# Rounding the second layer's context and weights inside the first layer's loop

## The reference, cut to what matters

```python
def bitnet_linear(x, W, b):
    w_scale = jnp.maximum(jnp.mean(jnp.abs(W)), 1e-05)
    qW = jnp.sign(W) * (jnp.abs(W) > 0.5 * w_scale).astype(W.dtype)
    i_scale = jnp.maximum(jnp.max(jnp.abs(x)), 1e-08) / 127.0
    qx = jnp.clip(jnp.round(x / i_scale), -128.0, 127.0)
    out = jnp.einsum('...i,oi->...o', qx, qW) * (w_scale * i_scale)
    return out + b
...
vis = bitnet_linear(dinov2_features, W_d2v, b_d2v)
image_embeds = bitnet_linear(vis, W_img, b_img)
fused = bitnet_linear(text_embeddings, W_txt, b_txt)
for Wa, ba in ((W_att0, b_att0), (W_att1, b_att1)):
    kv = bitnet_linear(image_embeds, Wa, ba)
...
x = _layernorm(x + _L0_attn_ref(x, ...), axis=-1)
x = _layernorm(x + _L0_xattn_ref(x, ctx_768, ...), axis=-1)
```

## Time and profile before

| What | us |
|---|---|
| median of 3 runs | 2812.44 (2810.92 to 2817.76) |
| profiled execution, its own time | 2813.72 |
| its span in the profile | 2812.4 |
| stage one, start to last copy | 0 to 242 |
| inputs of stage two, to the first copy of the values | 242 to 365 |

### The profile page before, as it was taken

How to read it: one execution, slowest core, us unless ns; L and a number is a source line. 1 busy time by engine, 2 the same in 40 slices (tenths; PEclk the granted TensorE clock), 3 DMA queues, 4 the chain that set the end, 5 groups by cost and what they waited for, 6 DMA issues and landing times. The chain is left out here.

```text
span 2812.4 us, 41641 instructions
## 1 busy us (share of the span) xinstructions
PE 2188.7 (78%) x15624; PEld 1422.1 (51%) x15694; DVE 1672.9 (59%) x3413; ACT 1179.7 (42%) x2185; POOL 567.4 (20%) x489
## 2 busy tenths in 40 slices
PE   6993689896408999277779999995887696788677
PEld 3552157673406888234435555653555443455544
DVE  4666965468763333456666666643777642777663
ACT  2222844335232333032225555563666443566443
POOL 2110000001273455401220000001322131322052
PEclk9996689998657999578889999996998898899999
DMA  3005000100260111233321011102000001000000
GB/s 111 1 1 156 15 1 1 46 1 1 76 230 28 46 46 42 68 88 85 93 77 36 25 36 25 25 13 90 1 1 1 11 1 60 1 1 1 37 12 23
DMA packets 75074, 113.30 MB, mean 40 GB/s; under 512 B 22916, under 2 KB 59744, under 8 KB 74208
## 3 DMA queue, kind: packets, MB, share of 16 engines
q1 hardware_dynamic: 71808, 102.24, 12.1%
q0 software_dynamic: 3072, 8.39, 0.9%
HBM read 85.38 MB, written 31.20 MB: 41 GB/s over the span
## 5 line engine op out<-in xcount | busy, mean ns | idle before, releaser
L2510 DVE TENSOR_REDUCE xa_max<-psum 128x1 f32<-128x1024 f32 (+1 forms) x256 | 248.4, 988 | 132.5 <-PE psum L2420 131.9
L2591 ACT ACTIVATE xa_work<-psum 128x1024 f32<-128x1024 f32 (+1 forms) x208 | 212.7, 1023 | 188.9 <-PE psum L2443 187.0
L2458 PE MATMUL psum<-xa_work,xa_values 128*33 128x128 f32 (+1 forms) x3328 | 223.9, 277 | 0.0
L2458 PEld LDWEIGHTS psum<-xa_work,xa_values 128*33 128x33 f32 (+1 forms) x3328 | 168.1, 111 | 73.7 <-issue 70.2
L2781 PE MATMUL psum<-wqkv_l,x_hl_l 128*128 128x512 bf16 x538 | 136.9, 400 | 65.7 <-POOL x_hl_l L3041 32.9
L3147 PE MATMUL psum<-h_ch_f,w_f 128*128 128x512 bf16 (+1 forms) x556 | 135.1, 397 | 34.3 <-issue 13.1
L1645 DVE TENSOR_SCALAR moe_raw<-psum,tile_b 128x256 f32<-128x256 f32 x184 | 78.3, 475 | 136.8 <-PE psum L1487 135.8
L1741 POOL TENSOR_TENSOR x_ch<-moe_raw,x_ch 128x512 bf16<-128x512 f32 x92 | 105.4, 1156 | 150.8 <-ACT x_ch L1701 148.7
L2443 PE MATMUL psum<-xa_query_rows,xa_key_rows 98*128 98x512 bf16 (+1 forms) x416 | 127.2, 388 | 8.4 <-ACT xa_work L2591 7.7
L1487 PE MATMUL psum<-moe_rows,moe_w 128*128 128x256 bf16 x1104 | 131.0, 277 | 3.0 <-POOL moe_rows L1737 3.0
L2420 PE MATMUL psum<-xa_key_rows,xa_query_rows 96*128 96x512 bf16 (+1 forms) x512 | 124.9, 339 | 8.8 <-ACT xa_work L2591 3.7
(11 more groups left out here) (441 smaller groups left out, 4824.0 us busy)
## 6 DMA issues: line engine op xcount, KB each, us to landing
xa_key_rows<-cross_keys SPq DMA_DIRECT2D x48, 200.1 KB, 3.4
moe_raw<-in_moe_w SPq DMA_DIRECT2D x16, 512.0 KB, 5.0
x_ch<-in_moe_w SPq DMA_DIRECT2D x16, 512.0 KB, 5.0
moe_rows<-slots_in SPq DMA_DIRECT2D x23, 256.0 KB, 2.8
slots_out<-moe_rows SPq DMA_DIRECT2D x23, 256.0 KB, 2.1
ctx_f<-in_ctxT SPq DMA_DIRECT2D x2, 2401.5 KB, 26.0
cross_keys<-xa_k_hl SPq DMA_DIRECT2D x6, 800.5 KB, 3.7
xa_ctx_f<-in_ctxT SPq DMA_DIRECT2D x4, 800.5 KB, 4.7
```

The lines of the kernel that those rows point to most:

```text
L2458: ins = pe.matmul(total.ap[a * LANE:a * LANE + VC, c:c + PIECE], t["v"][b][0:rows, kt, first + a, :], exps[0:rows, a, c:c + PIECE], start= ...
L2510: v.tensor_reduce(t["maxes"][n % 2][:, qt * HU + a, part:part + 1], u.wide[:, 0:c1 - c0], AX.X, ALU.max).then_inc(*u.free)
L2591: act.activation(t["exps"][k % EXPS][0:rows], u.wide[0:rows].rearrange("p (m q) -> p m q", q=T), ACT.Exp, scale=1.0 / float(np.sqrt(np.flo ...
```

## The change

- The plan of stage one gets 49 more entries (three of them pauses without work): for the weights five sums, one PE matmul and five ternary steps between the steps of batch one; then, evenly over all the rest of the plan, the maxima of 16 context chunks, the scale, and 16 roundings. A rounding is a multiplication on ACT followed by one DVE instruction on both halves of the chunk.
- The context is read twice from DRAM, in 32 transfers of some 308 KB (96 partitions, 2 halves, 400 or 401 columns of f32), into a ring of two chunk buffers. Each transfer from the third on is issued by SP once the chunk two before it has been read (first pass) or rounded (second pass).
- `x_step` has one buffer instead of two; raw weights lie in `sq_ch` and `g_wide`, the ternary temporary in `y_ch`, so ACT waits for the last ternary step before it first writes there.
- `settle` behind stage one now also waits for the last rounding.
- In stage two the maximum of the text comes first, beside the `d2v` matmuls, which need nothing more. The text is rounded in four groups among the maxima of `img`; its matmuls and its eight copies on ACT come beside the rounding for the keys. ACT's copies of `d2v` no longer write an accumulated sum.

```diff
@@ rwkv_plan @@
-    plan = flat(first[0:3]) + [("tables",)] + flat(first[3:])
+    start, plan = flat(first[0:3]) + [("tables",)] + flat(first[3:]), []
...
+    first_weights, later = early_steps()
+    n = next(k for k, step in enumerate(plan) if step[:2] == ("open", 1))
+    end = next(k for k, step in enumerate(plan) if step == ("center", 0, 0))
+    n = min(n, end)
+    return start + mingle(plan[:n], first_weights) + mingle(plan[n:] + flat(finish(B - 1)), later)
+def early_steps():
+    names, chunks = [name for name, _, _, _ in SMALL], range(len(CHUNKS))
+    weights = [("abs", name) for name in names] + [("ctx_max", 0), ("sums",)] + [("ternary", name) for name in names]
+    return weights, ([("ctx_max", c) for c in chunks[1:]] + [("ctx_col",), ("pause",), ("ctx_turn",), ("pause",), ("ctx_wide",), ("pause",)]
+                     + [("ctx_round", c) for c in chunks])
@@ rwkv_sp @@
+    for i in range(2 * n):
+        if i > n + 1:
+            sp.wait_ge(*s.cx_rounded(i - n - 1))
+        elif i > 1:
+            sp.wait_ge(*s.cx_read(i - 1))
+        c0, c1 = CHUNKS[i % n]
+        sp.dma_start(ctx_chunk(t, i), ctx[:, :, c0:c1]).then_inc(*ctx_chunk_loaded(s, i).up(16))
@@ early_dve (called by rwkv_dve) @@
+    elif kind == "ctx_max":
+        c, = step[1:]
+        v.wait_ge(*ctx_chunk_loaded(s, c)(16 * (c // 2 + 1)))
+        v.tensor_reduce(t["mcols"][0:CP, c:c + 1], ctx_chunk(t, c), AX.XY, ALU.max, apply_absolute_value=True).then_inc(*s.cx_read.up())
...
+    elif kind == "ctx_round":
+        c, = step[1:]
+        c0, c1 = CHUNKS[c]
+        v.wait_ge(*s.cx_scaled(c + 1))
+        v.tensor_scalar(t["q8"][0:CP, :, c0:c1], ctx_chunk(t, len(CHUNKS) + c), ROUND, ROUND, ALU.add, ALU.subtract).then_inc(*s.cx_rounded.up())
@@ rwkv_act @@
+        elif kind == "ctx_round":
+            c, = step[1:]
+            i = len(CHUNKS) + c
+            chunk = ctx_chunk(t, i)
+            act.wait_ge(*s.c_scaled(1))
+            act.wait_ge(*ctx_chunk_loaded(s, i)(16 * (i // 2 + 1)))
+            act.mul(chunk, chunk, t["inv"][0:CP, 0:1]).then_inc(*s.cx_scaled.up())
@@ bitnet_inputs_pe @@
+    outputs("d2v", CP, range(4), False)
     peak_pe(m, s, t, use, 1, 3)
+    outputs("d2v", CP, range(4, len(CHUNKS)), False)
+    peak_pe(m, s, t, use, 2, 1)
+    outputs("img", P, range(len(CHUNKS)), True)
+    peak_pe(m, s, t, use, 3, 2)
@@ bitnet_inputs_dve @@
+    v.tensor_reduce(t["mcols"][:, text:text + 1], m.x_ch[:], AX.XY, ALU.max, apply_absolute_value=True).then_inc(*s.v_step.up())
+    scale(3, text, text + 1, (("txt", 4),))
+    for c in range(len(CHUNKS)):
+        maxima("d2v", c)
+    scale(1, 0, 2 * len(CHUNKS), (("img", 1),))
+    rounded(1)
+    for c in range(len(CHUNKS)):
+        maxima("img", c)
+        if c % 4 == 3:
...
+                v.tensor_scalar(t["qx"][:, h, g * BANK:(g + 1) * BANK], x, ROUND, ROUND, ALU.add, ALU.subtract).then_inc(*s.text_rounded.up())
+    scale(2, 0, 2 * len(CHUNKS), (("att0", 2), ("att1", 3)))
+    rounded(2)
@@ bitnet_inputs_act @@
+    text = [(g, o) for g in range(4) for o in range(HALVES)]
+    for c in range(len(CHUNKS)):
+        multiplied(2, c)
+        if 4 <= c < 4 + len(text):
+            g, o = text[c - 4]
             u = use["text", g, o]
             act.wait_ge(*u.full)
             act.activation(t["fused"][:, o, g * BANK:(g + 1) * BANK], u.ap, ACT.Identity, scale=t["s_out"][:, 4:5],
```

More of the change, by code:

```diff
@@ L460, in rwkv_pe @@
             ins.then_inc(*u.fill)
+        elif kind == "sums":
+            u = use[step]
+            pe.wait_ge(*s.w_summed(len(SMALL)))
+            pe.wait_ge(*u.empty)
+            pe.matmul(u.ap[:, 0:8], m.const("ones"), t["wsum"][:], start=True, stop=True).then_inc(*u.fill)
+        elif kind == "ctx_turn":
+            u = use[step]
+            pe.wait_ge(*s.peak(1))
+            pe.wait_ge(*u.empty)
+            pe.transpose(u.ap[0:1, 0:P], t["mcols"][:, 39:40], m.const("ident")).then_inc(*u.fill)
+        elif kind == "ctx_wide":
+            u = use[step]
+            pe.wait_ge(*use["ctx_turn",].done)
+            pe.wait_ge(*u.empty)
+            pe.matmul(u.ap[:, 0:1], m.const("ones", 1), t["mone"][:], start=True, stop=True).then_inc(*u.fill)
         elif kind == "channels":
@@ L913, in bitnet_inputs_pe @@
             ins.then_inc(*u.fill)
-    for n, (name, rows) in enumerate((("d2v", CP), ("img", P))):
-        peak_pe(m, s, t, use, n + 2, n)
-        for c, (c0, c1) in enumerate(CHUNKS):
-            pe.wait_ge(*s.quantized(8 + 32 * n + 2 * c + 2))
-            for o in range(HALVES):
-                u = use[name, c, o]
-                pe.wait_ge(*u.empty)
-                for h in range(HALVES):
-                    ins = pe.matmul(u.ap[:, 0:c1 - c0], t["q_" + name][0:rows, h, o * P:(o + 1) * P], t["q8"][0:rows, h, c0:c1],
-                                    start=h == 0, stop=h == 1)
-                ins.then_inc(*u.fill)
-    peak_pe(m, s, t, use, 4, 2)
 def bitnet_inputs_dve(m, s, t, use):
@@ L930, in bitnet_inputs_dve @@
     text = 36
-    v.memset(t["wsum"][:], 0.0).then_inc(*s.zeroed.up())
-    v.memset(t["mcols"][:], 0.0).then_inc(*s.zeroed.up())
-    v.wait_ge(*s.zeroed(2))
-    v.tensor_reduce(t["mcols"][:, text:text + 1], m.x_ch[:], AX.XY, ALU.max, apply_absolute_value=True).then_inc(*s.v_step.up())
-    peak_dve(m, s, t, use, 3, text, text + 1)
-    v.wait_ge(*s.w_loaded(16 * 5))
-    for _ in ternary_dve(m, s, t, use, SMALL, 0, t["tmp"]):
-        pass
-    v.wait_ge(*s.ternary(5))
-    v.wait_ge(*s.scaled.now())
@@ L951, in bitnet_inputs_dve, with scale, rounded @@
+    def scale(slot, first, end, places):
+        peak_dve(m, s, t, use, slot, first, end)
         v.wait_ge(*s.scaled.now())
-        out_scale_dve(m, s, t, n, name, n)
-        if n == 2:
-            out_scale_dve(m, s, t, n, "att1", 3)
+        for wname, place in places:
+            out_scale_dve(m, s, t, slot, wname, place)
         v.wait_ge(*s.scaled.now())
+    def rounded(n):
         for c, (c0, c1) in enumerate(CHUNKS):
             for h in range(HALVES):
-                quantize_dve(m, s, t, n, t["q8"][0:rows, h, c0:c1], t["wide"][0:rows, h, c0:c1], rows, h and 4 + 16 * n + c + 1)
@@ L971, in bitnet_inputs_act, with multiplied @@
     act = m.nc.scalar
+    def multiplied(n, c):
+        c0, c1 = CHUNKS[c]
+        x = t["wide"][:, 1, c0:c1]
+        act.mul(x, x, t["inv"][:, n:n + 1]).then_inc(*s.scaled_in.up())
+    for c, (c0, c1) in enumerate(CHUNKS):
+        for o in range(HALVES):
+            u = use["d2v", c, o]
+            act.wait_ge(*u.full)
+            act.activation(t["wide"][:, o, c0:c1], u.ap[:, 0:c1 - c0], ACT.Identity, scale=t["s_out"][:, 0:1],
+                           bias=m.col("b_d2v", o)).then_inc(*u.free)
     act.wait_ge(*s.scaled(2))
```

232 lines of the change are left out of this document (146 added, 86 removed).

## The result

The changed kernel takes 2797.0 us (median of 4 runs, 2793.0 to 2800.5) against 2814.2 of the kernel before beside it (2810.9 to 2817.8): ratio 0.9941, 95% interval 0.9925 to 0.9957, some 17 us or 0.6% faster. The prediction was 2791 in a range of 2779 to 2804.

The account below looks back on a forecast made before the run. Stage one was taken as bound by PE, stage two's inputs by DVE. Profiled 2813.7 less 35.6 (stage two) plus 14.2 (stage one) gave 2792.3, the median 1.3 lower: 2791.0 us, range 2779 to 2804.

Parts of the forecast that it names:

- The four blocks: Stage two, DVE: weights, context maxima, its scale and its rounding leave, 9.7, 14.5, 2.2 and 16.3 us, together 42.55.
- the `d2v` maxima: Stage two: they end 1 us later than DVE alone would, behind ACT's copies and a slow PE; bounds 0 and 3.
- ACT's text copies: Stage two: eight text copies among ACT's multiplications delay the first copy of the values by 5.9 us; bounds 3 and 7.
- a stage one that ends behind 263: Sign of being wrong; the forecast had stage one end near 256 us.
- batch four: Stage one: 13 roundings wait for ACT's multiplications; PE's sum starts 3.3 us late, the last masked product 6.2; term +6.2.
- the walk: Stage one: new order followed along the old timeline, plan step by plan step, to price the waits added ahead of PE.
- the tail: End of stage one: rounding 14 and ACT's multiplication add 1.6 us, the last rounding ahead of `settle` 0.6.
- the clock term: Stage one: 1.0 us for PE's lower clock after three longer waits in batch four; bounds 0 and 7.
- The half-clock rival: Batch four's waits are paid at half clock, 5.8 us more, and some 4 in batches two and three: 2801; chance 15%.
- all but the tail is hidden: Rival: stage one hides all added work but its tail, 2.2 us: 2779; chance 14%.
- The ring: Rival: two chunk buffers too slow in batch four if a landing takes over 4.6 us; 2822 at 9.3; chance 9%.
- DVE never waits for a chunk's transfer: Sign of being right in the changed profile: chunk loads stay hidden, with a landing estimated at 3.6 us.

Follow-up runs that it names:

- Experiment 9: Changed kernel with the text's roundings spread over the second set of maxima and its matmuls and copies ahead of the last scale: ratio 0.9926.
- experiments 1 and 2: 1: changed kernel without stage one's added steps and their transfers, ratio 0.9877. 2: the same with two `x_step` buffers, ratio 0.9869.
- Experiment 6: Changed kernel with PE's waits behind the last batch filled with extra matmuls (three, four and four): ratio 0.9928.
- experiments 3 and 4: 3: changed kernel without the context's multiplications, roundings and second pass, ratio 0.9900. 4: changed kernel without ACT's sixteen multiplications only, ratio 0.9915.
- Experiment 8: Changed kernel with ACT's multiplication of each chunk half a slot of the plan ahead of DVE's rounding: ratio 0.9914.
- experiment 11: Changed kernel with text ahead of the last scale, PE filled and no roundings in the tail, DVE multiplying and rounding alone in two passes: ratio 0.9899.

## Why the prediction was right, and which term was mis-sized

**Stage two: right.** 38.0 us against 35.6. The four blocks were read from the earlier trace rows and left as priced. Of the two that take a part back, the `d2v` maxima cost nothing (1.0 taken, bounds 0 and 3), and ACT's text copies 5.45 - 0.85 = 4.6 (5.9 taken, bounds 3 and 7). 42.55 - 4.6 = 37.95. Experiment 9 shows the second by taking it away.

**Stage one: 8 us short in size, and by its own sign wrong.** 22.3 against 14.2 in the profiled executions, 18 to 20 by the times of experiments 1 and 2. The prediction named a stage one that ends behind 263 as a sign of being wrong, and it ended at 264.7 (264.3 in experiment 9). Three pieces, cut at the first and the last score of batch four, before:

```profile
0.00:150.30 150.30, 119.45 (x688) 67.85 (x688) 83.36 (x156) 35.77 (x77) 29.84 (x33) 0.94 0.15 52
150.30:209.50 59.20, 57.60 (x421) 35.33 (x420) 39.72 (x76) 11.77 (x22) 10.73 (x11) 1.00 0.01 1
209.50:242.40 32.90, 19.05 (x112) 14.20 (x108) 15.85 (x43) 5.13 (x10) 0.00 (x0) 0.81 0.00 0
```

and in the changed kernel:

```profile
0.00:157.70 157.70, 122.49 (x692) 67.91 (x692) 107.02 (x196) 35.80 (x77) 31.06 (x33) 0.94 0.31 91
157.70:225.50 67.80, 61.97 (x424) 38.44 (x423) 47.12 (x92) 21.25 (x33) 10.97 (x11) 0.92 0.19 50
225.50:264.70 39.20, 23.09 (x112) 17.27 (x108) 18.17 (x46) 9.40 (x15) 0.00 (x0) 0.67 0.09 26
```

The growth of a piece is split into PE's idle time (length less the second number), which the walk (the prediction's step-by-step sum) priced, and its busy time, which for the same matmuls is the clock's:

| Piece | longer | idle | walk | busy |
|---|---|---|---|---|
| batches one to three | 7.4 | 4.4 | 4.75 | 3.0 |
| batch four | 8.6 | 4.2 | 6.2 | 4.4 |
| the tail | 6.3 | 2.3 | 2.2 | 4.0 |
| all | 22.3 | 10.9 | 13.15 | 11.4 (1.0 taken) |

- Batches one to three: the first mix's four matmuls took 3.78 for 1.98 and the score behind them 2.08 for 1.13, 2.75 us at half clock and nearly all of the 3.0. The 1.0 for the two sums of weights was right (55.27 against 54.22).
- Batch four: one wait near 4 us was forecast, and PE waited 4.08. Its sum starts 12.2 late, of which batch four itself makes 4.9; 3.3 were forecast. Two of three roundings that took 1.10 to 1.29 us instead of the 0.58 priced stand ahead of it (the hardware, below). As a whole the idle time came out 2.0 us under the walk. Half clock behind the long wait adds 1.6 on the sum's row alone.
- The tail: the waits came out as priced. Experiment 6 gives back 5.4 us of it with nothing changed but PE's idling.

**The step that was mis-sized is the clock term:** 1.0 taken, bounds 0 and 7, and 11.4 measured (11.8 in experiment 9). The row on which it was sized was misread. The earlier trace rows showed full clock from 188 to 216 "with PE waiting three times", and I took that for a property of the place. But three of the waits there lasted half a microsecond and a fourth 2.4 us, and the wait that the prediction itself forecast there was 4 us. PE's waits between 188 and 216, before:

```profile
PE psum L419 <- DVE a_masked L546: 2.4, 1, 2.4
PE psum L458 <- DVE y_ch L567: 0.6, 1, 0.6
PE psum L445 <- ACT g_wide L657: 0.5, 1, 0.5
PE psum L436 <- ACT sq_ch L646: 0.5, 1, 0.5
```

The tail, at 0.77 in the earlier trace rows behind waits of 1.45, 2.14 and 2.17 us, was the row to size it by, and the longer waits there were forecast without a clock term of their own. The half-clock rival said 2801, the forecast 2791; 2797.0 lies between, and the rival's mechanism is in it, in part at other places: batches two and three had their slow stretch before and kept it, and the first mix and the tail, which the rival didn't name, have 6.8 of the 11.4 us.

**Luck.** The clock term alone was 10.4 us short. The total missed by 6.0 us only, since two errors went the other way: stage two gave 2.4 us more than forecast, and the walk priced 2.3 us of waiting too many. The forecast's own range was 2785 to 2797 with 11 to 17 us for stage one; the first was met at its edge and the second wasn't.

The Trainium skill ("TensorE: Matmul & The Clock Gate", "HAM oscillation — how this bites in real kernels") has bursts of matmuls between waits run at half clock, burst after burst. In the tail this case's rows agree (2.78, 3.78 and 6.56 us in turn, and 1.85, 2.05 and 3.62 with the fillings); at the first mix a wait of 4.05 us was followed by half clock every time, and one of 2.55 us by either clock.

**The other rivals.** That all but the tail is hidden falls with experiments 3 and 4. The ring: chunks landed in 3.0 us (3.6 estimated, 4.6 would have decided). But "DVE never waits for a chunk's transfer" was wrong once by 1.6 us, and ACT waited 7.3 us in three places. A ring of three wasn't tried, so what these waits cost isn't shown. Transfer lines of the page:

```profile
ctx_chunk<-in_ctxT SPq DMA_DIRECT2D x24, 300.0 KB, 3.0
...
ctx_chunk<-in_ctxT SPq DMA_DIRECT2D x8, 300.8 KB, 3.0
```

**Why two operations so short cost 12 us** is shown by 3, 4 and 8 in outline: DVE alone had room, but a piece of its queue waited for a piece of ACT's that stood behind a square, and the next square waited for DVE. Experiment 8, which leaves both engines their work, gets 4.6 us of the 12.3 back by the end. Whether the rest is ACT's own time, the ring or the clock stays open, and experiment 11, which was to separate DVE's own time, left it undecided.

## What to carry to other kernels

Work that is moved into idle time of two engines should not make one wait for the other at the same place of their plans: put the first engine's part half a slot ahead (4.6 us by the end here). Price every new wait ahead of PE twice, as its length and as the matmuls behind it at half clock, and size the second from a stretch whose waits are as long as the new ones, not from one with short waits. Compare a stretch before and after at its new place, since everything behind a delay has moved. For a change of 5 us, read idle and busy time of the stage apart and take the times of several runs as well: the same stage repeated within 0.4 us once, but two stages with the same matmuls came out at 242.5 and 247.6, and the same code behind them anywhere from 2434 to 2449.

## What the hardware showed that was not expected

A rounding of 96x800 f32 into bf16 took 0.57 us in 13 places and 1.10, 1.11 and 1.29 in three. In these three POOL was already multiplying when the rounding started: POOL ran from 193.86 to 194.90, the rounding from 194.23 to 195.33; POOL from 199.51 to 200.55, the rounding from 199.87 to 200.98; POOL from 210.20 to 211.24, the rounding from 210.39 to 211.68. The rounding ended 0.43 or 0.44 us behind POOL's end, as if it had stood still until then.

```profile
210.20 1.04 POOL L821 TENSOR_TENSOR r_heads<-r_ch,head_of_half 128x512 f32<-128x512 f32 x1 [9.65 <-PE psum L451]
210.39 1.29 DVE L701 TENSOR_SCALAR ctx_q<-ctx_chunk 96x800 bf16<-96x800 f32 x1 [2.46 <-ACT ctx_chunk L790]
```

Where the rounding starts first, it isn't slowed, as in experiment 4:

```profile
197.89 0.56 DVE L702 TENSOR_SCALAR ctx_q<-ctx_chunk 96x800 bf16<-96x800 f32 x1
198.29 1.06 POOL L815 TENSOR_TENSOR r_heads<-r_ch,head_of_half 128x512 f32<-128x512 f32 x1 [3.47 <-PE psum L451]
```

Experiment 8 has both orders: a rounding that started 0.11 us ahead of POOL took 0.58, one that started 0.05 us behind it took 1.42 and again ended 0.43 behind POOL's end.

The Trainium skill ("SBUF — State Buffer", "SBUF: two separate sides") says that DVE (in its two-port fast modes, or with two inputs from SBUF against a GpSimd instruction that reads SBUF) and GpSimd share one port pair, which whoever comes first holds for a whole instruction. These rows agree. No experiment took POOL's multiplication away, so the port is not shown as the reason by an edit; that the order of the two starts decides is read from rows of eight profiles.
